# Perceiver layer on one core: layer norm statistics moved to the context stage, the first attention tile ahead of the last norms, key copies split

## The reference, cut to what matters

```python
# x: 64 batches of 64 tokens of 256; context: 64 batches of 256 rows of 192
v = layernorm(x) @ Wv.T + bv ; t = context @ Wt.T + bt            # both to 128
x = x + (v @ t.T) / max(norm(v) * norm(t), 1e-8)                  # 256 cosines per token, added to the token
q, k, v = projections(layernorm(x))                               # 16 heads of 16, with biases
o = softmax(q @ k.T / 4) @ v                                      # within a batch of 64 tokens
o = o - (sum(o * v) / (sum(v * v) + 1e-8)) * v                    # per head
x = x + o @ wo.T + bo
h = layernorm(x) ; e = argmax(h @ router) ; p = softmax(h @ router)[e]     # 14 experts
x = x + p * (gelu(h @ w1[e] + b1[e]) @ w2[e] + b2[e])
```

## Time and profile before

| | us |
|---|---|
| median of 3 runs | 570.13 |
| lowest and highest | 568.34 and 572.67 |
| the profiled execution | 573.11 |
| its span, first to last instruction | 571.1 |
| TensorE busy | 517.0 (91%) |
| VectorE busy | 353.2 (62%) |
| ScalarE busy | 349.6 (61%) |
| POOL busy | 253.8 (44%) |

### The profile page before, as it was taken

The page is one execution under the profiler, slowest core; times in us unless marked ns, Lnnn a source line. Parts: engine busy times, 40 slices in busy tenths (PEclk is TensorE's granted clock), DMA queues, the critical chain, the costliest instruction groups (busy, mean ns, idle before and its releaser), DMA issues. The chain is left out here.

```text
span 571.1 us, 14797 instructions
## 1 busy us (share of the span) xinstructions
PE 517.0 (91%) x4323; PEld 399.8 (70%) x4324; DVE 353.2 (62%) x1036; ACT 349.6 (61%) x835; POOL 253.8 (44%) x436
## 2 busy tenths in 40 slices
PE   7999999968999999999999999852499999999993
PEld 5455555556777777778777777641399999999993
DVE  3676554446999999999899898855023332333331
ACT  2667777648888888888888888821143333333330
POOL 2454432343445665766657676525123233323332
PEclk9999999989999999999999999975599999999998
DMA  8864436001112333333331111104656666666650
GB/s 313 289 226 153 147 129 197 2 10 34 30 29 58 97 111 109 92 98 94 107 110 47 47 33 43 45 20 176 192 176 206 207 196 209 207 210 186 206 168 9
DMA packets 43981, 71.61 MB, mean 125 GB/s; under 512 B 15770, under 2 KB 32031, under 8 KB 43808
## 3 DMA queue, kind: packets, MB, share of 16 engines
q1 hardware_dynamic: 40048, 62.29, 35.9%
q0 software_dynamic: 3456, 8.53, 4.0%
q10 hardware_dynamic: 432, 0.26, 0.2%
HBM read 54.21 MB, written 11.60 MB: 115 GB/s over the span
## 5 line engine op out<-in xcount | busy, mean ns | idle before, releaser
L1154 PEld LDWEIGHTS psum<-arena,ring 128*128 128x128 f32 x640 | 78.7, 195 | 4.7 <-ACT arena L923 1.8
L1154 PE MATMUL psum<-arena,ring 128*128 128x128 f32 x640 | 80.3, 280 | 1.0 <-ACT arena L923 1.0
L923 ACT ACTIVATE arena<-psum 128x256 f32<-128x256 f32 x40 | 15.4, 385 | 104.9 <-PE psum L942 104.9
L807 DVE TENSOR_TENSOR arena<-psum,arena 128x256 f32<-128x256 f32 x40 | 17.0, 425 | 97.6 <-PE psum L1166 97.6
L1166 PE MATMUL psum<-w_s,arena 128*128 x320 | 75.9, 381 | 0.0
L1166 PEld LDWEIGHTS psum<-w_s,arena 128*128 128x128 f32 x320 | 57.6, 190 | 6.3
L883 ACT ACTIVATE arena<-kT 16x256 f32<-16x256 f32 x128 | 52.7, 412 | 1.1
L496 POOL TENSOR_TENSOR token_of<-arena,zero_u 128x1 uint32<-128x1 uint32 x40 | 8.9, 222 | 94.8 <-DVE arena L812 89.5
L500 POOL DMA_INDIRECT out<-arena,token_of x40 | 39.8, 994 | 20.1 <-POOL token_of L496 16.1
L1055 PEld LDWEIGHTS psum<-xnT,wk_s 128*128 128x128 f32 x256 | 31.8, 195 | 22.5 <-ACT xnT L889 14.6
L436 POOL TENSOR_TENSOR ov<-o_n,v_s 128x256 f32<-128x256 f32 x32 | 23.6, 738 | 53.0 <-DVE o_n L609 53.0
(11 more groups left out here) (172 smaller groups left out, 1176.0 us busy)
## 6 DMA issues: line engine op xcount, KB each, us to landing
ring<-w SPq DMA_DIRECT2D x40, 512.0 KB
w_s<-ctxT SPq DMA_DIRECT2D x15, 768.0 KB, 4.4
w_s<-w SPq DMA_DIRECT2D x16, 448.0 KB, 3.5
arena<-routed SPq DMA_DIRECT2D x40, 132.0 KB
tok<-x SPq DMA_DIRECT2D x16, 256.0 KB, 4.7
v_swap<-v_s SPq DMA_DIRECT2D x64, 64.0 KB
arena<-kT SPq DMA_DIRECT2D x128, 16.0 KB
routed<-pad_rec SPq DMA_DIRECT2D x1, 1980.0 KB, 10.7
```

Of the source, the lines that this page charges most:

```text
L1154: mm = pe.matmul(bank(4 + p)[:, f * P:(f + 1) * P], w1_s[:, k % 4, c * F + f * P:c * F + (f + 1) * P], xgT[:, p, c * P:(c + 1) * P], start ...
```

## The change

Nine edits in all:

- VectorE takes the statistics of the attention's layer norm in the context stage, a pair at a time (`b = j - 1`): two `bn_stats` behind the `bn_aggr` of the first layer norm and ahead of the norms, two `bn_aggr` behind the copy of the value norms. The wait for `vnorm_sbuf` moves ahead of the norms.
- POOL makes epsilon, mean, power and product for the pair in the context step, ahead of the sum into `tok`.
- `mean`, `vareps`, `rstd` and `std` are kept for all 32 tiles, and these pieces leave the attention step on both engines.
- The normalisation of tile t waits for `std_ok`, and only in steps written out; tile 1's is done with tile 0's.
- On ScalarE and TensorE `attention_step(-1)` moves into `context_step(NB-1)`, on TensorE in the place where the next pair's transposes would stand.
- `attention_step(0)` comes ahead of `context_step(NB)` on TensorE, ahead of `context_step(NB-1)` on VectorE and POOL, and ahead of `context_step(NB+1)` on ScalarE.
- `context_step` gets one more step on VectorE and POOL, behind `attention_step(1)`.
- ScalarE's copy of the transposed `xn` stands between the second and the third of its key copies.
- SP loads the second pair of `x` ahead of the larger part of the first context.

```diff
-        mv = sb("mv", [P, 2, 2])
-        vareps = sb("vareps", [P, 2, 1])
-        rstd = sb("rstd", [P, 2, 1])
+        mv = sb("mv", [P, 2, 2, 2])
+        mean = sb("mean", [P, NT])
+        vareps = sb("vareps", [P, NT])
+        rstd = sb("rstd", [P, NT])
...
                     sp.dma_start(ctx_in_sb[:, 0, 0:2 * SC], ctxT[0, :, 0:2 * SC]).then_inc(s["ctx_head_in"], 16)
+                    load_x(1, 1)
                     sp.dma_start(ctx_in_sb[:, 0, 2 * SC:CW], ctxT[0, :, 2 * SC:CW]).then_inc(ctx_in[0], 16)
-                    load_x(1, 1)
...
+                b = j - 1
+                if paired(b):
+                    pair = bass.ds(b * 2, 2)
+                    need(pool, s["stats_ok"], b + 1)
+                    pool.tensor_tensor(vareps[:, pair], mv[:, 1 - p, :, 1], eps[:, :].broadcast_to([P, 2]), ALU.add)\
+                        .then_inc(s["vareps_ok"], 1)
+                    pool.tensor_copy(mean[:, pair], mv[:, 1 - p, :, 0])
+                    need(pool, s["vareps_ok"], b + 1)
+                    pool.tensor_tensor(rstd[:, pair], vareps[:, pair], mhalf[:, :].broadcast_to([P, 2]), ALU.pow)\
+                        .then_inc(s["rstd_ok"], 1)
+                    need(pool, s["rstd_ok"], b + 1)
+                    pool.tensor_tensor(std[:, pair], vareps[:, pair], rstd[:, pair], ALU.mult).then_inc(s["std_ok"], 1)
...
-                if live(n):
-                    p = k % 2
-                    need(pool, s["stats_ok"], n + 1)
-                    pool.tensor_tensor(vareps[:, p], mv[:, p, 1:2], eps[:, :], ALU.add).then_inc(s["vareps_ok"], 1)
...
-                if live(n):
-                    need(pool, s["vareps_ok"], n + 1)
-                    need(pool, s["xn_ok"], n - 1)
-                    pool.tensor_tensor(rstd[:, p], vareps[:, p], mhalf[:, :], ALU.pow).then_inc(s["rstd_ok"], 1)
-                    need(pool, s["rstd_ok"], n + 1)
-                    need(pool, s["l1_ok"], n - 3)
-                    pool.tensor_tensor(std[:, (k + 2) % 4], vareps[:, p], rstd[:, p], ALU.mult).then_inc(s["std_ok"], 1)
...
-            run_steps(pool, context_step, -4, NB - 3, 6, 10)
-            attention_step(-2, 2)
-            context_step(NB - 3, NB - 3)
-            attention_step(-1, 3)
-            context_step(NB - 2, NB - 2)
-            context_step(NB - 1, NB - 1)
+            run_steps(pool, context_step, -4, NB - 1, 6, 10)
             pool.wait_ge(s["consts_in"], 16 * RESTS)
             pool.wait_ge(s["consts_made"], CONSTS)
-            run_steps(pool, attention_step, 0, NT + 9, RLO, RHI, RING)
+            attention_step(0, 0)
+            context_step(NB - 1, NB - 1)
+            attention_step(1, 1)
+            context_step(NB, NB)
+            run_steps(pool, attention_step, 2, NT + 9, RLO, RHI, RING)
...
+                b = j - 1
+                if paired(b):
+                    need(dve, s["tok_sum"], b + 1)
+                    for h in range(2):
+                        raw = dve.bn_stats(stats[:, h, :], rows(b * 2 + h))
+                    raw.then_inc(s["stats_raw"], 1)
                 if paired(j):
                     need(dve, s["dots_psum"], j + 1)
                     need(dve, s["norms_log"], j - 1)
+                    need(dve, s["vnorm_sbuf"], j + 1)
...
                 if paired(v):
                     need(dve, s["vnorm_psum"], v + 1)
+                    need(dve, s["stats_raw"], b + 1)
+                    need(dve, s["std_ok"], b - 1)
                     dve.tensor_copy(vnorm[:, p, :], bank(1)[:, 2 * P:2 * P + 2]).then_inc(s["vnorm_sbuf"], 1)
-                    need(dve, s["vnorm_sbuf"], v + 1)
+                if paired(b):
+                    if isinstance(b, int):
+                        need(dve, s["stats_raw"], b + 1)
+                        need(dve, s["std_ok"], b - 1)
+                    for h in range(2):
+                        whole = dve.bn_aggr(mv[:, p, h, :], stats[:, h, :])
+                    whole.then_inc(s["stats_ok"], 1)
...
+                def normalise(t, p):
+                    if isinstance(t, int):
+                        need(dve, s["std_ok"], t // 2 + 1 if t < RLO else NB)
                     need(dve, s["xT_psum"], t - 1)
-                    dve.tensor_scalar(xn[:, p, :], rows(t), mv[:, p, 0:1], rstd[:, p], ALU.subtract, ALU.mult)\
-                        .then_inc(s["xn_ok"], 1)
+                    dve.tensor_scalar(xn[:, p, :], rows(t), mean[:, bass.ds(t, 1)], rstd[:, bass.ds(t, 1)],
+                                      ALU.subtract, ALU.mult).then_inc(s["xn_ok"], 1)
+                if live(t) and not (isinstance(t, int) and t == 1):
+                    normalise(t, (k + 1) % 2)
+                if isinstance(i, int) and i == -1:
+                    normalise(1, 1)
...
-                if live(n):
-                    q = k % 2
-                    if isinstance(n, int):
-                        need(dve, s["tok_sum"], n // 2 + 1, NB)
-                    need(dve, s["vareps_ok"], n - 1)
-                    dve.bn_stats(stats[:, q, :], rows(n)).then_inc(s["stats_raw"], 1)
-
-                    need(dve, s["stats_raw"], n + 1)
...
-                if live(n):
-                    dve.bn_aggr(mv[:, q, :], stats[:, q, :]).then_inc(s["stats_ok"], 1)
...
-            run_steps(dve, context_step, -4, NB - 3, 2, 10)
-            attention_step(-2, 2)
+            run_steps(dve, context_step, -4, NB - 3, 6, 10)
+            attention_step(-1, 3)
             context_step(NB - 3, NB - 3)
-            attention_step(-1, 3)
             context_step(NB - 2, NB - 2)
+            dve.wait_ge(s["consts_made"], CONSTS)
+            attention_step(0, 0)
             context_step(NB - 1, NB - 1)
-            dve.wait_ge(s["consts_made"], CONSTS)
-            run_steps(dve, attention_step, 0, NT + 5, RLO, RHI, RING)
+            attention_step(1, 1)
+            context_step(NB, NB)
+            run_steps(dve, attention_step, 2, NT + 5, RLO, RHI, RING)
...
                 if live(i):
 
                     need(act, s["k_ok"], i + 1)
+                    spread_keys((0, 2))
                 if live(t):
                     need(act, s["xT_psum"], t + 1)
                     need(act, s["val_psum"], t - 1)
                     act.activation(xnT[:, 1 - p, :], bank(5, D), ACT.Copy).then_inc(s["xT_ok"], 1)
+                if live(i):
+                    spread_keys((4, 6)).then_inc(s["kd_ok"], 1)
...
-            attention_step(-1, 3)
-            context_step(NB, 0)
-            context_step(NB + 1, 1)
+            run_steps(act, context_step, -1, NB, 4, 12)
+            context_step(NB, NB)
             act.wait_ge(s["consts_in"], 16 * RESTS)
             act.wait_ge(s["vd_ones"], 9)
-            run_steps(act, attention_step, 0, NT + 5, RLO)
+            attention_step(0, 0)
+            context_step(NB + 1, NB + 1)
+            run_steps(act, attention_step, 1, NT + 5, RLO)
...
+                if isinstance(n, int) and n == NB:
+                    pe.wait_ge(s["t_sbuf"], NB - 1)
+                    attention_step(-1, 3)
...
-            attention_step(-1, 3)
-            context_step(NB, NB)
+            run_steps(pe, context_step, -1, NB, 4, 12)
             pe.wait_ge(s["consts_made"], CONSTS)
             attention_step(0, 0)
+            context_step(NB, NB)
```

More of the change, by code:

```diff
@@ L213, in build @@
         rec = sb("rec", [P, RING, REC])
-        std = sb("std", [P, 4, 1])
+        std = sb("std", [P, NT])
         l1 = sb("l1", [P, GROUP, E])
@@ L426, in attention_step @@
             def attention_step(i, k):
-                y, w, x, n = i - 3, i - 4, i - 9, i + 2
+                y, w, x = i - 3, i - 4, i - 9
                 if live(x):
@@ L580, in attention_step @@
             def attention_step(i, k):
-                t, n, u, y, w, z = i + 1, i + 2, i - 1, i - 3, i - 4, i - 5
+                t, u, y, w, z = i + 1, i - 1, i - 3, i - 4, i - 5
                 r = (k - 4) % RING
@@ L703, in attention_step @@
                 if live(i):
-                    need(dve, s["std_ok"], i + 1)
-                    dve.scalar_tensor_tensor(l1[:, k % GROUP, :], bank(6)[:, D:DX], std[:, k % 4], lbias[:, :],
+                    dve.scalar_tensor_tensor(l1[:, k % GROUP, :], bank(6)[:, D:DX], std[:, bass.ds(i, 1)], lbias[:, :],
                                              ALU.mult, ALU.add).then_inc(s["l1_ok"], 1)
@@ L846, in context_step @@
                     act.activation(tsq[:, p, :], both, ACT.Square, bias=xbt_s).then_inc(s["t_sbuf"], 1)
-            run_steps(act, context_step, -1, NB, 4, 12)
             def attention_step(i, k):
@@ L877, in attention_step, with spread_keys @@
                     act.activation(oT[:, q, :], bank(5, D), ACT.Copy).then_inc(s["oT_ok"], 1)
-                if live(i):
-                    need(act, s["k_ok"], i + 1)
-                    for h in range(0, HC, 2):
+                def spread_keys(heads):
+                    for h in heads:
                         r = slice(h * HD, (h + 1) * HD)
```

(6 more changed lines are left out.)

3 lines of the change are left out of this document (removed).

## The result

The changed kernel took 555.26 us (median of 4 runs, 554.13 to 556.28) against 569.56 for the kernel before; the ratio is 0.9741, 95% interval 0.9695 to 0.9786. The forecast was 564.0: faster, as said, but by 14.3 us and not by 6.1. The profiled span fell from 571.1 to 554.5.

What follows compares the result with a forecast made beforehand. TensorE was taken to bound the context stage and, within 0.15 us, the ring's light steps. 573.1 - 0.8 + 0.3 - 6.2 - 1.0 + 1.6 = 567.0, on the median's footing 564.0 us; range 554.0 to 569.5.

Steps and rivals of the forecast that it cites:

- Start: Kernel start: x's second pair, loaded earlier, no longer queues behind 512 KB; 0.8 us saved, the rounded-up middle of 0 to 1.44.
- Context stage: Context stage: VectorE's added statistics fit into idle time except in four early steps; 0.3 us lost, bounds 0 and 3.3.
- The rival in which VectorE becomes the bound: Context stage: normalisation stretched beside POOL's new block, statistics' time missing in some 14 steps; 580 us, chance 0.06.
- Turn: Passage from context to attention: tile 0's work fills TensorE's wait for cos; 6.2 us saved, bounds 2.5 and 7.5.
- Ring: Attention steps: 1.0 us saved before the scatters begin, then 1.6 lost through held signals.
- VectorE's loop of 7.93 takes TensorE's place as the bound: Light steps beside scatters: rsum, scatter, held signal, smax, rsum takes 7.93 us, as in tile 30's step.
- light step: Attention step without the gathering of router logits or settling of positions; 7.73 us before, TensorE busy for 7.58.
- I take the first: Ring: of two ends, held signals (1.6 lost) or no hold (5.4 won), it chose held signals, chance 0.52.
- the forecast's case without hold: Rival for the ring: no held signals in the new places, 5.4 us won; 560.0, or 557.0 by the median, chance 0.30.
- The 5.4 groups: Ring from 193.5 to 359 us, in groups of two light steps, a gathering and a settling one; 31.6 us each before.
- a gathering and a settling one: Steps gathering four tiles' router logits and settling their positions: 7.77 and 8.39 us before, forecast 8.4 and 7.63.
- TensorE's own 7.58 is the floor: 0.15 a light step: Ring, xnT between the keys: 0.15 us saved per light step, 1.0 over seven steps (tiles 4 to 10) before scatters.

Runs made afterwards that it cites:

- chips 6 and 7: The kernel after, unchanged, run again as a control on two chips with late signals: 560.39 us (0.9776) and 561.44 us (0.9758).
- chip 13: Further chip without such late signals, both kernels unchanged: the kernel after took 554.94 us (0.9709), ring 201.91; the kernel before had a ring of 209.57.
- the corners: Four kernels, scatter behind xn's transposes, statistics old or moved, keys together or split: 570.60 (neither), 566.19 (split), 561.01 (statistics) on chip 13; 554.77 (both) on chip 7.

## Why the forecast was right in direction and wrong in size

*Start.* Forecast 0.8 saved, measured 1.6. The middle between 0 and 1.44 was too low, and 1.44 wasn't the upper end: the later part of the first context, which I charged with a part of the gain, is there in time for TensorE in the first profile (L974 follows at 8.68), and the third pair comes 0.5 closer behind the second.

*Context stage.* Forecast 0.3 lost, measured 0.2: one early step of 6.78 for 6.59. The rival in which VectorE becomes the bound fell: 40.00 of 40 us of TensorE's time are busy.

*Turn.* Forecast 6.2, measured 6.45, 6.1 of it by the order as seen when it was undone. Its steps came true too. The turn begins 1.8 us earlier; with that added, tile 1's projections stand at 120.1 (forecast near 120), the last sum into tok ends at 124.6 (124.88) and the first probabilities are transposed at 128.3 (near 128). One step was off without cost: tile 0's work ends at 118.5 in the forecast and the last norms at 120.4, where the row it reads has 2.5 us for them.

*Ring.* Forecast 0.6 longer; measured 10.2 shorter, and this is the step that failed: "VectorE's loop of 7.93 takes TensorE's place as the bound" in each light step. In the profile after, the scores' signal isn't held, smax is taken at once, and light steps take 7.41 to 7.52 with TensorE as the bound. Three things in it, in order of size:

- "I take the first" of the two ends, the one with held signals. The late signals are real: chips 6 and 7 show them at the very place forecast, scores and smax. But the first profile of before has them and the first of after has none, which the forecast couldn't know; by their signals the two came from chips, or sessions, of different kinds. On chip 13, which has none, the ring goes from 209.57 to 201.91, 7.7 shorter; the forecast's case without hold had 1.0 + 5.4 = 6.4. (The 5.4 groups overlap with the seven steps: 20 steps are left behind them, 5.0 groups, so it should have been 5.0, and the 1.6 of the first case 1.5.)
- The price with late signals. Forecast for two light steps, a gathering and a settling one: 7.93, 7.93, 8.4, 7.63 = 31.9. On chip 6 they are 7.73, 7.84, 7.75 and 7.65 = 30.97. The settling step is right. The light step is 0.1 to 0.2 too dear. The gathering step was off by 0.65, by a matter of 0.1 us: the forecast had the scatter start 0.10 behind the start of xn's transposes (239.3 and 239.20), with their signal held. On chip 6 it starts 0.23 behind, and ScalarE takes the signal at 229.28 as if there were no scatter:

```profile
228.81 0.44 PE L959 MATMUL psum<-ident,xn 128*128 128x128 f32 x2
229.04 1.08 POOL L472 DMA_INDIRECT routed<-rec,pos  x1 [0.18 <-issue]
...
229.28 0.38 ACT L903 ACTIVATE xnT<-psum 128x256 f32<-128x256 f32 x1 [0.43 <-issue]
```

- "TensorE's own 7.58 is the floor: 0.15 a light step". Light steps go down to 7.41, and the split gives 0.28 a step (7.69 to 7.41, seen alone ahead of the first scatter). The busy time of the light step was read as work; in it the first projection after the wait for xnT is longer too, 1.16 for 1.05.

That VectorE's part is worth something only in the settling step was nearly right in the corners (0.4 to 0.7 there, 0.15 in the gathering step), but not in the kernel after as it is, where its return also lengthened the steps behind the settling ones by 0.3. GpSimd's operations are put at nothing in the forecast. With them back the ring is 3.2 to 3.6 longer (210.10 on chip 11 against 206.5 and 206.9 on chips 6 and 7), with other signals late than in the kernel after; that the place of the scatter is the reason is argued, not shown, since no run without late signals has them alone.

The forecast also read the hold too narrowly: "all but one of the late signals stand on the same transposes". In the ring of that first profile 16 signals of xn's transposes are over 0.1 us late, light steps included, and so are 16 of the weighted values (L1105).

*The sum.* Where signals are late, -1.6 + 0.2 - 6.4 - 5.4 = -13.2, measured 12.7 and 13.8 between the medians on chips 6 and 7. Where they aren't, -1.6 + 0.2 - 6.4 - 7.7 = -15.5, measured 16.0 on chip 13. The 14.3 of the first comparison lies between. So even on a chip as the forecast assumed, the kernel takes 560 to 561 and not 564, and the gain is over twice the 6.1 forecast. That a profile without late signals answered the forecast is chance; that it priced the start and the light step too low is not.

*The rule.* The Trainium skill (SBUF — State Buffer, "Who interferes with whom") has TensorE and ScalarE never wait on anyone. TensorE's own matmuls weren't slowed: from the first start of a tile's scores to the last goes 0.72 us beside a scatter and without one, with late signals and without. But its signals landed up to 1.3 us late beside a scatter on four chips, and ScalarE and VectorE, and through them TensorE, waited for that. Whether the ports of which the section speaks have a part in it, no run here shows. The time without late signals, which the forecast drew from that rule, fits the first profile of after and those of chip 13.

## What to carry to other kernels

Before pricing a stall that one profile shows, profile the same kernel on a second chip: here 2.5 us of the ring before and 4.8 to 5.0 of the ring after went with the chip. Where an engine's transfers by index can delay other engines' signals, start them just behind the last signal that the critical engine's step waits for; a wait that costs that engine only idle time does it. When the copy that the bounding engine needs next stands behind copies that nobody needs yet, put it between them, and expect its worth to show only once the other limits of the step are gone (4.1 became 6.3 here).

## What the runs showed of the hardware

On chips 4, 6, 7 and 11 most signals of TensorE due between about 0.3 and 1.35 us behind the start of a GpSimd indirect scatter are late: 26 of 29 in the ring of the kernel after on chip 6, 31 of 32 in that of before on chip 7. Most land 1.25 to 1.8 behind that start. A few due 0.13 to 0.25 or about 1.4 behind are late too. The place alone doesn't decide it: with VectorE's two operations back, on chip 11, the turned `o_f` due 0.59 to 0.64 behind 16 scatters was taken on time all 16 times, while on chip 6 all 13 due 0.68 to 1.07 behind were late. The scatter's instruction takes 0.96 to 1.31, as a rule 1.01 to 1.08, and in 27 of 32 cases the first packet of its queue moves 1.58 or more behind its start. On chip 13 the same programs show next to none of the lateness. I don't know the mechanism: neither the addresses nor the core were varied.
